# The load of the next block's chunk issued ahead of the store in SyncE's row phases

## What is computed

```python
x = inputs.reshape(b, G, h // G, t, s)          # G = 1, M = 16, I = 2
wI = w + jnp.eye(w.shape[-1], dtype=w.dtype)
ret = jnp.einsum('BGMTS,GMN->BGNTS', x, wI)
hq = jnp.einsum('BGMTS,BTGIM->BGITS', x, qw1)
ret = ret + jnp.einsum('BGITS,BTGIM->BGMTS', hq, qw2)
hk = jnp.einsum('BGMTS,BSGIM->BGITS', x, kw1)
ret = ret + jnp.einsum('BGITS,BSGIM->BGMTS', hk, kw2)
ret = ret + x * qdd.transpose(0, 2, 3, 1)[:, :, :, :, None]
ret = ret + x * kdd.transpose(0, 2, 3, 1)[:, :, :, None, :]
```

## Time and profile before

| what | value |
|---|---|
| median of 3 runs | 790.46 us (788.18 to 796.9) |
| the profiled execution | 788.75 us |
| its span | 785.3 us |
| mean granted clock of TensorE | 0.965 |
| busy: TensorE matmuls, VectorE, ScalarE, GpSimd | 695.1, 540.1, 509.2, 497.0 us |
| chain that ended last: TensorE, DMA, issue, VectorE, SyncE's queue | 64%, 10%, 10%, 7%, 6% |
| DMA | 159.03 MB, mean 203 GB/s |
| loads of x | 128, of 512 KB, 5.8 us from issue to landing (median) |
| stores of the result | 128, of 512 KB, 4.5 us from issue to landing (median) |

### The profile page before, as it was taken

One profiled execution on the slowest core, in us unless ns is written; L12 is line 12 of the kernel. 1 busy time (PEld: TensorE's weight loads), 2 busy tenths in 40 slices (PEclk: granted clock), 3 DMA queues, 4 the chain that ended last, 5 costly groups with the idle time before them and its releaser, 6 DMA issues.

```text
span 785.3 us, 41859 instructions
## 1 busy us (share of the span) xinstructions
PE 695.1 (89%) x18088; PEld 642.3 (82%) x18088; DVE 540.1 (69%) x770; ACT 509.2 (65%) x945; POOL 497.0 (63%) x464
## 2 busy tenths in 40 slices
PE   9759899899997899987998999879899879999976
PEld 5658798788987789977887989879898879888975
DVE  5375666566875669766776668657686666866797
ACT  7846577656775667754766567666676557766753
POOL 2757676558665776656765676557766567656632
PEclk6978999999999999999999899999999999999999
DMA  7992559833897339955498438774399654983055
GB/s 166 228 253 59 137 209 328 252 96 111 296 330 202 105 104 362 280 173 137 182 320 256 126 111 296 268 243 124 96 349 277 190 135 152 340 269 103 7 212 214
DMA packets 78564, 159.03 MB, mean 203 GB/s; under 512 B 42048, under 2 KB 43072, under 8 KB 76224
## 3 DMA queue, kind: packets, MB, share of 16 engines
q1 hardware_dynamic: 78408, 156.59, 63.3%
HBM read 87.22 MB, written 69.34 MB: 199 GB/s over the span
## 4 chain that ended last, share of the span: by engine, by line
PE 64%; DMA 10%; issue 10%; DVE 7%; SPq 6%; POOL 2%; ACT 1%; DVEq 0%; ACTq 0%; POOLq 0%
PE PB L856 22%; PE PB L808 15%; PE PA L785 14%; PE PA L827 14%; DMA X<-in_x_dram 9%; DVE OUT L671 3%; DVE WB L256 2%; SPq L293 2%; DVE Y L647 2%; POOL WA L248 1%; SPq L289 1%; SPq L296 1%; SPq L274 1%; SPq L284 1%; SPq L278 1%
## 5 line engine op out<-in xcount | busy, mean ns | idle before, releaser
L856 PE MATMUL PB<-Y,WB 128*128 128x128 f32 x2048 | 270.0, 282 | 12.1 <-DVE OUT L671 7.3
L856 PEld LDWEIGHTS PB<-Y,WB 128*128 128x128 f32 x2048 | 243.6, 189 | 25.2 <-issue 18.0
L647 DVE TENSOR_TENSOR Y<-PB,Y 128x512 f32 (+1 forms) x256 | 165.6, 690 | 100.8 <-PE PB L808 93.9
L485 ACT ACTIVATE Y<-PA 128x512 f32<-128x512 f32 (+1 forms) x240 | 137.2, 630 | 117.3 <-PE PA L785 117.1
L256 POOL TENSOR_TENSOR WB<-RT,mask 128x512 f32<-128x512 f32 x128 | 143.2, 1119 | 109.7 <-PE PB L856 107.5
L493 ACT ACTIVATE X<-PA 128x512 f32 (+1 forms) x256 | 140.2, 606 | 99.1 <-PE PA L827 99.1
L248 POOL TENSOR_TENSOR WA<-RS,mask 128x512 f32<-128x512 f32 x128 | 134.1, 1048 | 82.6 <-PE PA L827 56.8
L785 PE MATMUL PA<-X,WA 64*64 64x64 f32 x7680 | 151.4, 227 | 34.3 <-DMA X<-in_x_dram 20.7
L808 PE MATMUL PB<-X,WB 64*64 64x128 f32 x4096 | 162.2, 281 | 16.6 <-issue 11.9
L785 PEld LDWEIGHTS PA<-X,WA 64*64 64x64 f32 x7680 | 132.9, 138 | 51.8 <-DMA X<-in_x_dram 23.1
L517 ACT ACTIVATE OUT<-X 64x512 f32<-64x512 f32 (+1 forms) x256 | 161.1, 629 | 20.4 <-DMA out_dram<-OUT 13.7
(11 more groups left out here) (40 smaller groups left out, 164.5 us busy)
## 6 DMA issues: line engine op xcount, KB each, us to landing
X<-in_x_dram SPq DMA_DIRECT2D x128, 512.0 KB, 5.8
out_dram<-OUT SPq DMA_DIRECT2D x128, 512.0 KB, 4.5
RT<-products SPq DMA_DIRECT2D x120, 128.0 KB, 3.3
products<-PROD SPq DMA_DIRECT2D x16, 128.0 KB, 7.4
Y<-in_right_dram SPq DMA_DIRECT2D x8, 128.0 KB, 10.6
X<-in_right_dram SPq DMA_DIRECT2D x8, 128.0 KB, 18.6
RT<-products SPq DMA_DIRECT2D x8, 96.0 KB, 5.0
QP<-in_rows_dram SPq DMA_DIRECT2D x8, 80.0 KB, 3.6
```

The costliest lines, as they stand in the source:

```text
L485: nc.scalar.activation(rows_of(Y, k, j)[:, :, WIDE * h:WIDE * (h + 1), :].rearrange("q a s c -> q a c s"), PA[HALVES * (j % RING) + h].rea ...
L647: nc.vector.tensor_tensor(at, by_columns(PB[HALVES * (g % RING) + h]), at, ALU.add).then_inc(b_done, 1)
L856: last = nc.tensor.matmul(PB[g % SLOTS][:, COLS * r:COLS * (r + 1)], WB[:, g % SLOTS, P * r:P * (r + 1)], rows_of(Y, k, t2_chunk(o))[:, (i ...
```

## The change

In `t_phase` of SyncE the store and the load behind one wait change places. It applies to o = 0 to 12 of the seven blocks that have a next one. What each of them waits for, moves and signals stays as it is.

```diff
             def t_phase(k, more, params):
                 for o in range(CHUNKS):
+
                     sp.wait_ge(b_done, t2_done(k) + PER_CHUNK * (o + 1))
-                    store(k, o)
                     if more and o + SLACK < CHUNKS:
                         load_x(k + 1, o + SLACK)
+                    store(k, o)
                     if more and o == PROD_STORE:
```

## The result

The changed kernel is slower: 809.04 us (805.45 to 812.45, 6 runs) against 790.51 us of the kernel before in the same comparison (782.64 to 796.9, 6 runs); ratio 1.0265, 95% interval 1.0226 to 1.0305. The prediction was 778.5 us, faster. The profiled execution of the changed kernel has a span of 809.5 us where that of before had 785.3.

The account below looks back on a forecast made before the run. TensorE was taken to be bound partly by late loads of x at block ends. Gains 12.3 + 3.0 (clock) - 3.3 (code) = 12.0 us gave 776.8 us profiled, 778.5 us median; range 770 us less 2 us of scatter to 787 us.

Parts of the forecast that it names:

- Where x is late: TensorE waits for x ahead of the last chunk's matmuls at seven row-phase ends, together 14.9 us.
- How much earlier the last load lands: Last load of each row phase: 2.5 us earlier at ends 1 to 4, 1.9 at 5 to 7; 12.3 us gained.
- the 0.54 us of the issue: In SyncE's queue at the last pair, the load takes the store's place and is issued 0.54 us earlier.
- the sign of a wrong queue term: At block ends, no store ahead should save the load 2.0 or 1.4 us; wrong if it still needs 5.5 us or more.
- of which 7 matter by the above. Nothing is added or removed: Of 91 store-load pairs in the row phases only the 7 last ones count; SyncE's queue and bytes stay.
- ring of four slots: Output slots ScalarE copies into: reused after 10.15 us, later stores need 10.1 at worst, so cost 0.
- took back 3.3 us: Deduction for late TensorE code: the whole gain of ends 1 and 7 (2.3 us) and 1.0 us of the others'.
- rival (b): At most block ends TensorE stops for code instead of x; perhaps 5 us and 1 of clock left, 784.5 us; chance 0.14.
- sign of being wrong on the code: At the block ends, TensorE's "issue" waits ahead of s1 at more than two ends would show the code estimate wrong.
- The slower rival (d): Stores land too late for their OUT slot, each chunk step 0.5 us longer, kernel 45 us slower, 836 us; chance 0.04.
- The clock: After ends 3, 4 and 6 shorter idle time no longer lowers the granted clock; 0.7, 1.3 and 1.0, together 3.0 us.

Follow-up runs that it names:

- prod_later: Kernel before, store still first, but products stored and row parameters loaded after the pair of o = 12 instead of 11; 769.8 us, ratio 0.979, repeated 773.9 us, 0.978.
- prod_later_load_first: prod_later with the load directly ahead of the store in all 13 pairs; 807.4 us, ratio 1.025 to the kernel before.
- last_only: Kernel before with the load ahead of the store at the last pair (o = 12) alone, the other twelve unchanged; 780.7 us, ratio 1.000.

## Why the prediction was wrong

**Where x is late: right.** Seven waits at the block ends, 14.9 us, and they are worth that: prod_later, which removes nearly all of them with the order of before, gains 14 and 15 us of the medians it is compared with.

**How much earlier the last load lands: right in the middle, not at each end.** At the seven ends it needs 4.9, 4.4, 6.8, 4.4, 4.7, 4.1 and 5.6 us after the change, in the median 4.7, and 5.8, 6.3, 5.6, 6.2, 6.0, 6.1 and 4.7 before, in the median 6.0. With the 0.54 us of the issue it is 1.8 us earlier in the median instead of 2.5 and 1.9. At ends 3 and 7 it needed longer than before from its issue (6.8 and 5.6 us), which is over the 5.5 us that I had named as the sign of a wrong queue term. The waits for x all but went there too (0 and 0.46 us), at end 3 because TensorE, stopped for code at 348.18 us, arrived later. The Trainium skill, DMA: Bandwidth & Descriptors, "Queues, rings and completion order", has descriptors consumed in ring order on each engine, and that agrees with the load gaining in the median (6.0 to 4.7 us) when the store goes behind it.

**The failed step: "of which 7 matter by the above. Nothing is added or removed".** I counted 91 pairs and gave the 84 others no price, because their loads have three chunk steps and their stores a ring of four slots. Both covers held: 0.7 us of waits for x after 95 us in all, and none for a slot in a row phase with loads. But loads and stores are not the only traffic. TensorE's code comes through the same engines with 2.7 us to spare in a row phase, and of that 2.1 us were in use before. The change moved the median start by 0.9 us, past the edge, at 72 pieces. That costs 20.8 us in the row phases where it stands alone (prod_later_load_first) and 23.2 here (13.9 to 37.1). In the same trace the waits for x gave 14.8 back, so of 23.2 us 8.4 are left, and the row phases came out 14.9 us longer; of the other 6.5 us some 4.4 are longer matmul records and about 1.3 idle times under 0.3 us, so here too most of it is no stop.

**The code was in the sum, but as a cap on the gain.** I read the 1.83 us of issue at the first end as code that is late "by itself" and took back 3.3 us, and rival (b) let it eat half of the gain. It never had a term for code that the change makes later. Its own sign of being wrong on the code, issue ahead of s1 at more ends than two, came true: in the trace after s1 stops for issue at ends 1, 4, 6 and 7 (163.05, 445.89, 638.40 and 732.78 us). The first sign was there: a total of 43.9 us of issue waits ahead of TensorE in the trace of before, three times the waits for x at the ends, with DMA engines at a share of 0.99. A wait that large, on a supply that near its limit, needed a price for what the change does to it.

**The slower rival (d) named the wrong resource.** It had the stores late for their slot. They did get later (median 4.5 to 5.9 us, longest 7.6 to 8.6) and the slots never ran out.

**The clock.** Its fall at ends 3, 4 and 6 went: the granted clock is 1.00 in the stretches after these ends. The mean rose from 0.965 to 0.980 between the two profiled executions, but executions of the kernel before alone range from 0.961 to 0.980, so the rise of the mean can't be put down to the change.

**Open.** Why a store directly behind a load holds the code back, when the same store 1.3 us later or ahead of the load does not, the records don't show. The bytes are the same, and what the DMA engines do inside is not in the trace. Open too is how much of last_only's gain is real, and why the stops in the column phases scatter by over 10 us (24.4 and 37.4 us in the two executions of prod_later) between executions of one kernel.

## What to carry to other kernels

Before moving a transfer, list everything that goes through the DMA engines in that phase, the program's own code too. If an engine shows issue waits that recur at one place of its code, measure how far that supply is from its limit, and price what the move does to it at every repetition, not only at the place that the move is for. Where one transfer is late, move what delays it (here the products, one line, 0.978) before changing the order of a steady stream that works.

## What the hardware showed that I had not expected

- Two 512 KB transfers issued 0.55 us apart behave differently by their order towards a third party: load then store starts TensorE's next piece of code 3.0 us after the boundary, store then load 2.1. With gaps of 1.3 us or more it is 1.9 to 2.1 in either order.
- A piece of code needs 2.4 us in the median from the start of its packet to the first instruction, and the packet starts 0.7 to 0.8 us after the boundary when the row phases' loads are small. So of the 5 us that a piece lasts, some 3.1 are gone even where the DMA engines' share is about 0.6. This is an estimate: the 2.4 us are measured at stops, and those kernels have none in row phases.
- Loads and stores of the row phases at full size cost 1.2 us and more of a landing time each to the other: a load 5.2 to 5.8 us against 4.0 beside small stores, a store 4.5 to 5.9 against 3.3 beside small loads.
